# Expert tiles of 128 gathered rows in place of 256, in a routed feed-forward layer

## The chip, the cores and the metric

The kernel runs on 1 core of one Trainium2 chip. The metric is the device time of one execution in microseconds. Before the change the median of 3 runs is 1785.74 us (1784.13 to 1794.47).

## The reference

One block over x of shape (4, 1024, 128), 4096 tokens of width 128, in float32: attention, a feed-forward layer with experts, a state-space scan, and the same feed-forward layer with the same weights again, each on a layer norm of its input and added to it. The change touches the feed-forward layer:

```python
def _L0_ffn_ref(x, sw1, sw2, sw3, ew1, ew2, ew3, rw, rb):
    shared = silu(x @ sw1) * (x @ sw2) @ sw3
    probs = softmax(x @ rw + rb)                  # 8 experts
    w, idx = top_k(probs, 2); w = w / sum(w)
    h = silu(x @ ew1[e]) * (x @ ew2[e])           # 128 -> 256 per expert
    routed = sum over the two chosen e of w * (h @ ew3[e])
    return shared + routed
```

(The matrix products are written as `@` here; the reference computes all experts for all tokens and multiplies by gates that are zero for those not chosen.)

## The kernel before, in words

`build` writes out the stages one behind the other: projection, attention, a second attention branch (`memory`), the first feed-forward layer (`ffn`, stage "ffn1"), the scan ("ssm"), and the second feed-forward layer ("ffn2") with a final `join`. Within a stage each engine has its own program; engines wait for each other by semaphores, and a stage's end waits for all of them.

A feed-forward layer has two parts. `route` (L1576) goes over 8 units of 512 tokens: it normalises them, computes the shared part, picks two experts per token, counts for each pick its place in the expert's region, and POOL scatters the normalised rows with an indirect DMA (`scatter`, L1539; 64 DMAs of 128 rows) into `ex`, a buffer in DRAM with a region for each expert. Each row carries its token number and its gate in two more columns. Zero rows are stored behind each region's end. DVE then writes two small tables (`name_experts`, L1825, and `name_rows`, L1848): for each tile of the next part the expert whose weights it uses and the first row that it reads.

`run_experts` (L1861) goes over `TILES_EX` = 40 tiles of `ROWS` = 256 rows (`SUB` = 2 pieces of 128). That number is fixed: 8192 picked rows make 32 full tiles, and each of the 8 experts may need one more for its remainder. Every tile is computed, those that no expert needs too. The work on a tile:

```python
if on[2]:
    e = pe.value_load(at_expert[0:1, number_of(ti, tq)])
    pe.wait_ge(hid_ready, now(s - 2))
    ...
if on[1]:
    pe.wait_ge(xT_ready, now(s + 0))
    pe.wait_ge(w12_ready, now(s + 0))
    ...
if on[0]:
    pe.wait_ge(loaded[q], now(i * 16 + 16))
```

`pipeline` (L1893) writes the first `AHEAD` steps out, puts the rest into a loop whose turn is `AHEAD` steps, and writes out the last three. In the loop the counts that a step waits for are held in registers (`Turns`, L82; `now`, L131), which L111 and L1953 work out.

Of the kernel before, what the change touches and what calls it, by code (L numbers as in the profile page):

```python
# [30 lines left out]
UPT = UNIT // P  # L31
# [1281 lines left out]
EXPERTS, HIDDEN, TOP = 8, 256, 2  # L1313
HC = HIDDEN // P
TILES_IN = N // P
SUB = 2
ROWS = SUB * P

TILES_EX = TOP * N // ROWS + EXPERTS
# [6 lines left out]
XROW = D + 2  # L1326
TOKEN, GATE = D, D + 1
PADROW = TOP * N
AHEAD = 8
OUTS = 8  # L1330
UNITS_IN = N // UNIT
DEEP = 8
GROUP_ENDS = [1, 3, 5, UNITS_IN]
AHEAD_UNITS, AHEAD_ENDS = 2, [1, 2, 3, 5, 7, UNITS_IN]
EXPERT_STRIDES = [AHEAD, 16, SUB * 16]

def past(s, n):
# [21 lines left out]
class Router:  # L1360
# [22 lines left out]
    def signals(self):  # L1383

        m = self.m
        self.x_loaded = [m.sem(f"x_ld{k}") for k in range(DEEP)]
        self.r_loaded, self.ready, self.set_up, self.stat, self.mean = (m.sem(n) for n in ("r_ld", "ready", "set_up", "stat", "mean"))
# [25 lines left out]
def mean_dve(nc, r, dve, u):  # L1413
    k = u % DEEP
    dve.wait_ge(r.x_loaded[k], u // DEEP * 16 + 16)
    dve.wait_ge(r.mean, u * UPT)
# [11 lines left out]
def norm_dve(nc, r, dve, u):  # L1428
    k = u % DEEP
    dve.wait_ge(r.rstd_ready, sum(end <= u for end in r.ends) + 1)  # L1430
    if u >= DEEP:
        dve.wait_ge(r.sent[k], u // DEEP * (TOP * UPT * 16))
        dve.wait_ge(r.xT_made, u - DEEP + 1)
# [105 lines left out]
def scatter(nc, r, dram, pool, u, j):  # L1539

    k = u % DEEP
    if j == 0:
        pool.wait_ge(r.xn_ready, u * UPT + UPT)
        pool.wait_ge(r.twin_ready, u + 1)
        pool.wait_ge(r.id_ready, u + 1)
        pool.wait_ge(r.gate_ready, u + 1)
        pool.wait_ge(r.pos_ready, u + 1)
    n, j = j // UPT, j % UPT
    nc.gpsimd.indirect_dma_start(dram["ex"], bass.IndirectOffsetOnAxis(ap=r.pos[k][:, n, j:j + 1], axis=0),
                                 r.xn[k][:, n, j, :], None).then_inc(r.sent[k], 16)  # L1550

def rstd_pool(nc, r, pool, g):
# [22 lines left out]
def route(nc, dram, c, a, stage, src, w, w_loaded, t, r):  # L1576

    with ExitStack() as ctx:
        m = Mem(nc, ctx, stage)
        if r is None:  # L1580
            r = Router(m, dram[stage + "_sent"], GROUP_ENDS)
            r.signals()
        first = len(r.x)
# [5 lines left out]
        base = [m.sb(f"base{k}", [P, UPT, D]) for k in range(2)]  # L1589
        zeros = m.sb("zeros", [P, PADS * SUB, XROW])  # L1590
        counti = m.sb("counti", [1, EXPERTS], I32)
# [44 lines left out]
        def pads(eng, sem, experts):  # L1636
            for e in experts:
                n = eng.value_load(counti[0:1, e:e + 1], min_val=0, max_val=N)
                eng.dma_start(dram["ex"][ds(n + e * REGION, ROWS), :].rearrange("(j p) d -> p j d", p=P),
                              zeros[:, e * SUB:(e + 1) * SUB, :]).then_inc(sem, 16)  # L1640

        with nc.Block(no_gpsimd_drain=True) as block:
            @block.sync
            def _(sp):
# [15 lines left out]
                sp.wait_ge(r.ready, 7)  # L1660
                sp.dma_start(dram["ex"][IDLE:ROWS_EX, :].rearrange("(j p) d -> p j d", p=P), zeros[:, EXPERTS * SUB:, :]).then_inc(pads_stored[0], 16)
                for u in range(UNITS_IN):
# [95 lines left out]
            @block.gpsimd  # L1758
            def _(pool):
                if not first:  # L1760
                    set_up_pool(nc, r)
                pool.wait_ge(r.ready, 5)
                group, held = first, first - 1
                if not first:
                    nc.gpsimd.memset(zeros[:], 0.0).then_inc(r.ready, 1)
                if first:
                    for j in range(0, 3):
                        scatter(nc, r, dram, pool, held, j)
                rstd_pool(nc, r, pool, group)
                nc.gpsimd.iota(t["tile"][:], pattern=[[1, TILES_EX], [0, EXPERTS]], base=0, channel_multiplier=0,  # L1770
                               allow_small_or_imprecise_dtypes=True).then_inc(made, 1)
                nc.gpsimd.iota(t["enum"][:], pattern=[[0, TILES_EX], [1, EXPERTS]], base=0, channel_multiplier=0,
                               allow_small_or_imprecise_dtypes=True).then_inc(made, 1)
                nc.gpsimd.memset(t["onesv"][:], 1.0).then_inc(made, 1)
                nc.gpsimd.iota(t["idle"][:], pattern=[[ROWS, TILES_EX]], base=IDLE - FULL * ROWS, channel_multiplier=0,
                               allow_small_or_imprecise_dtypes=True).then_inc(made, 1)
                if first:
                    for j in range(3, 6):
                        scatter(nc, r, dram, pool, held, j)
                rstd_pool(nc, r, pool, group + 1)  # L1780
                if first:
                    nc.gpsimd.memset(zeros[:], 0.0).then_inc(r.ready, 1)
                pool.wait_ge(r.ready, 6)
                nc.gpsimd.iota(zeros[:, :, TOKEN].bitcast(I32), pattern=[[P, PADS * SUB]], base=PADROW, channel_multiplier=1).then_inc(r.ready, 1)
                if first:
                    for j in range(6, TOP * UPT):
                        scatter(nc, r, dram, pool, held, j)
                for u in range(first, UNITS_IN):
                    for j in range(TOP * UPT):
                        scatter(nc, r, dram, pool, u, j)  # L1790
                    if group + 2 + u - first < len(r.ends):
                        rstd_pool(nc, r, pool, group + 2 + u - first)
                for k in range(DEEP):
                    pool.wait_ge(r.sent[k], UNITS_IN // DEEP * TOP * UPT * 16)
        m.leave()
        if r.m is not m:
            r.m.leave()
# [63 lines left out]
def run_experts(nc, dram, c, stage, w, w_loaded, t, base, base_loaded):  # L1861

    with ExitStack() as ctx:
        m = Mem(nc, ctx, stage)
        at_expert, firsti = t["at_expert"], t["firsti"]
        x = [m.sb(f"x{q}", [P, SUB, XROW]) for q in range(AHEAD)]
        xT = [m.sb(f"xT{q}", [P, ROWS]) for q in range(2)]
        w12 = [m.sb(f"w12{q}", [P, 2 * HIDDEN]) for q in range(2)]
        act1 = [m.sb(f"act{q}", [P, HC, ROWS]) for q in range(2)]  # L1870
        hid = [m.sb(f"hid{q}", [P, HC, ROWS]) for q in range(2)]
        out = [m.sb(f"out{q}", [P, SUB, D]) for q in range(OUTS)]
        ps_x = [m.ps(f"ps_x{q}", [P, UNIT]) for q in range(2)]
        ps_h = [[m.ps(f"ps_h{n}{q}", [P, HC, ROWS]) for q in range(2)] for n in range(2)]
        ps_o = [m.ps(f"ps_o{q}", [P, UPT, D]) for q in range(2)]
        step, passed = m.sem("step"), m.sem("passed")
        loaded = [m.sem(f"loaded{q}") for q in range(AHEAD)]
        sent = dram[stage + "_sent"]
# [5 lines left out]
        def number_of(i, q):  # L1884

            return ds(i * AHEAD + q, 1) if not isinstance(i, int) else slice(i * AHEAD + q, i * AHEAD + q + 1)

        def shifted(i, q, by):

            at = q + by  # L1890
            return i + at // AHEAD, at % AHEAD

        def pipeline(body, turns, eng, lag):  # L1893

            deepest = max(lag)
            for s in range(AHEAD):
                body(0, 0, s, [g <= s for g in lag])
# [7 lines left out]
        with nc.Block(no_gpsimd_drain=True) as block:  # L1906
# [76 lines left out]
            def _(act):  # L1983
                turns = Turns(act, stage + "_act", EXPERT_STRIDES, first=1)

                def body(i, at, q, on):
                    s = i * AHEAD + q
                    if on[2]:
                        z, (ti, tq) = (q - 3) % 2, shifted(i, q, -3)
                        act.wait_ge(o_done, now(s - 2))  # L1990
                        if past(s, 3 + OUTS):
                            ui, uq = shifted(i, q, -3 - OUTS)
                            act.wait_ge(sent[uq], now(ui * (SUB * 16) + SUB * 16))
                        for j in range(SUB):
                            nc.scalar.activation(out[tq % OUTS][:, j, :], ps_o[z][:, j, :], ACT.Copy,  # L1995
                                                 scale=x[tq][:, j, GATE:GATE + 1]).then_inc(out_ready, 1)
# [14 lines left out]
            @block.gpsimd  # L2011
            def _(pool):
                m.wipe(pool)
                turns = Turns(pool, stage + "_pool", sorted(set(EXPERT_STRIDES + [SUB * AHEAD])), first=1)

                def body(i, at, q, on):
                    s = i * AHEAD + q
                    for j in range(SUB):
                        pool.wait_ge(out_ready, now(s * SUB + (j + 1)))
                        pool.sem_inc(passed, 1)  # L2020
                        nc.gpsimd.indirect_dma_start(dram["ey"], bass.IndirectOffsetOnAxis(ap=x[q][:, j, TOKEN:TOKEN + 1].bitcast(I32), axis=0),  # L2021
                                                     out[q % OUTS][:, j, :], None).then_inc(sent[q], 16)

                pipeline(body, turns, pool, [0])
                for q in range(AHEAD):
                    pool.wait_ge(sent[q], TILES_EX // AHEAD * SUB * 16)
# [52 lines left out]
def routing_scratch(nc, m, dram, stages):  # L2079

    for name, shape, dt in (("ex", (ROWS_EX, XROW), F32), ("ey", (PADROW + PADS * ROWS, D), F32), ("base", (N, D), F32)):
        dram[name] = nc.dram_tensor(f"{name}_dram", shape, dt).ap()
    for stage in stages:
        dram[stage + "r_sent"] = [m.sem(f"{stage}_sent{k}") for k in range(DEEP)]
        dram[stage + "e_sent"] = [m.sem(f"{stage}_out{q}") for q in range(AHEAD)]

# [836 lines left out]
```

## Time and profile before

| | us |
|---|---|
| median of 3 runs (lowest, highest) | 1785.74 (1784.13, 1794.47) |
| the profiled execution | 1792.23 |
| its span, first to last instruction | 1790.5 |
| PE busy in the span | 1362.6 (76%) |
| DVE busy | 1266.3 (71%) |
| POOL busy | 880.4 (49%) |
| ACT busy | 855.2 (48%) |
| first expert stage, from the first load (L1916) to the start of the last scatter (L2021) | 841.2 to 964.8 |
| second expert stage, from the first xT copy (L2007) to the start of the last scatter | 1643.9 to 1764.1 |

The times of the trace are in microseconds from the span's start. A row for a group of instructions gives the line, the engine, the operation, the tile written and the tiles read, and how many there are.
### The profile page before, as it was taken

How to read it: one execution, taken by the hardware profiler on the slowest of the kernel's cores; microseconds unless marked ns; L12 is line 12 of the kernel's file. 1: busy time of each engine (PE TensorE's matmuls, PEld its weight loads, DVE VectorE, ACT ScalarE, POOL GpSimd, SP SyncE). 2: the span in 40 equal slices, each digit the busy share in tenths (PEclk: the TensorE clock that was granted, in tenths of full speed). 3: DMA queues.
4: the chain of work that ended last, by engine and by line, in shares of the span. 5: the costliest groups of instructions: out<-in, count | busy, mean ns of one | idle time of the engine just before them, and what ended most of it. 6: DMA issues, size and time to landing. Idle time of an engine off the chain costs nothing. (4 is left out here: it accounts for less than half of the span.)

```text
span 1790.5 us, 27815 instructions
## 1 busy us (share of the span) xinstructions
PE 1362.6 (76%) x8207; PEld 677.6 (38%) x8208; DVE 1266.3 (71%) x2981; ACT 855.2 (48%) x1215; POOL 880.4 (49%) x775
## 2 busy tenths in 40 slices
PE   3448999999999898785995777586676544584993
PEld 1213333333333265553994232131221200353992
DVE  3666899999989267674333279998998999573343
ACT  3403666666666734221553668467476332121551
POOL 3400212121211454675665248869869666475662
PEclk9655999999999999997997888698788656797996
DMA  4821111111112232254333395976957863624336
GB/s 121 265 73 48 53 49 55 47 58 44 61 47 65 54 84 84 86 159 108 85 93 111 98 226 154 249 182 162 245 131 199 198 163 94 174 87 124 111 93 166
DMA packets 218312, 210.68 MB, mean 118 GB/s; under 512 B 49247, under 2 KB 188482, under 8 KB 215874
## 3 DMA queue, kind: packets, MB, share of 16 engines
q1 hardware_dynamic: 196174, 180.70, 37.7%
q0 software_dynamic: 9216, 19.02, 3.3%
q10 hardware_dynamic: 12800, 9.46, 1.8%
q8 instruction: 60, 0.98, 0.2%
q14 instruction: 62, 0.51, 0.1%
HBM read 145.27 MB, written 63.37 MB: 117 GB/s over the span
## 5 line engine op out<-in xcount | busy, mean ns | idle before, releaser
L804 ACT ACTIVATE attn_prob<-attn_ps_cols 128x1024 f32<-128x1024 f32 (+1 forms) x320 | 292.0, 940 | 219.7 <-PE attn_ps_cols L680 218.7
L2546 POOL TENSOR_TENSOR ssm_hc<-ssm_h,ssm_cb 128x1024 f32<-128x1024 f32 x128 | 300.5, 2355 | 136.1 <-DVE ssm_h L2529 112.3
L2529 DVE TENSOR_TENSOR_SCAN ssm_h<-ssm_decay,ssm_ps_u 128x1024 f32<-128x1024 f32 x128 | 292.7, 2287 | 29.9 <-ACT ssm_decay L2517 12.6
L830 POOL TENSOR_SCALAR_AFFINE_SELECT attn_prob<-attn_prob 128x512 f32<-128x512 f32 x128 | 81.2, 635 | 415.7 <-ACT attn_prob L804 415.7
L712 DVE CUSTOM_DVE_ANT_0 attn_ps_rows<-attn_ps_rows,const_mask_rows 128x384 f32<-128x384 f32 (+3 forms) x512 | 236.1, 522 | 39.5 <-PE attn_ps_rows L647 37.3
L647 PE MATMUL attn_ps_rows<-attn_ks,attn_qs 72*128 72x512 bf16 (+3 forms) x768 | 228.8, 351 | 44.3 <-DMA attn_qs<-parts_dram 31.0
L2517 ACT ACTIVATE ssm_decay<-ssm_wide,ssm_aneg 128x1024 f32<-128x1024 f32 x128 | 146.1, 1146 | 173.5 <-DVE ssm_h L2529 97.1
L2480 PE MATMUL ssm_ps_u<-ssm_stack,ssm_spread 96*128 96x512 bf16 x256 | 99.1, 479 | 154.0 <-DVE ssm_h L2529 147.4
L680 PE MATMUL attn_ps_cols<-attn_qs,attn_ks 75*128 75x512 bf16 (+3 forms) x768 | 194.3, 333 | 4.6 <-DMA attn_qs<-attn_nrows 3.9
L699 PE MATMUL attn_ps_o<-attn_prob,attn_vw 128*32 128x512 f32 (+3 forms) x1536 | 166.6, 506 | 0.3 <-POOL attn_prob L830 0.3
L717 DVE TENSOR_REDUCE attn_nm<-attn_ps_rows 128x1 f32<-128x512 f32 x256 | 157.8, 682 | 7.8 <-PE attn_ps_rows L647 7.7
L2524 DVE TENSOR_TENSOR ssm_ps_u<-ssm_ps_u,ssm_bb 128x1024 f32<-128x1024 f32 x128 | 154.8, 1209 | 8.7 <-PE ssm_ps_u L2480 8.7
L647 PEld LDWEIGHTS attn_ps_rows<-attn_ks,attn_qs 72*128 72x128 bf16 x768 | 71.4, 100 | 180.4 <-DVE attn_nm L712 65.0
L2480 PEld LDWEIGHTS ssm_ps_u<-ssm_stack,ssm_spread 96*128 96x128 bf16 x256 | 17.3, 103 | 252.9 <-DVE ssm_h L2529 202.7
L680 PEld LDWEIGHTS attn_ps_cols<-attn_qs,attn_ks 75*128 75x128 bf16 x768 | 69.9, 100 | 87.8 <-ACT attn_prob L804 35.5
L2021 POOL DMA_INDIRECT ey_dram<-ffn1e_out,ffn1e_x x80 | 76.6, 957 | 50.9 <-ACT ffn1e_out L1995 38.3
L2021 POOL DMA_INDIRECT ey_dram<-ffn2e_out,ffn2e_x x80 | 76.6, 957 | 50.1 <-ACT ffn2e_out L1995 37.5
L2496 PE MATMUL ssm_ps_y<-ssm_hc,ssm_gather 128*32 128x512 f32 x512 | 83.4, 782 | 7.6 <-POOL ssm_hc L2546 7.6
L1970 PE MATMUL ffn1e_ps_h<-ffn1e_xT,ffn1e_w 128*128 128x256 f32 x320 | 77.6, 386 | 0.9 <-ACT ffn1e_xT L2007 0.9
L1970 PE MATMUL ffn2e_ps_h<-ffn2e_xT,ffn2e_w 128*128 128x256 f32 x320 | 77.1, 384 | 0.9 <-ACT ffn2e_xT L2007 0.9
L1096 DVE TENSOR_TENSOR mem_am<-mem_ps_a,const_strict 128x512 f32<-128x512 f32 x96 | 60.3, 684 | 20.6 <-PE mem_ps_a L1014 20.5
L1940 DVE TENSOR_TENSOR ffn1e_hid<-ffn1e_act,ffn1e_ps_h 128x512 f32<-128x512 f32 x40 | 27.5, 688 | 66.0 <-PE ffn1e_ps_h L1970 66.0
(361 smaller groups left out, 2438.6 us busy)
## 6 DMA issues: line engine op xcount, KB each, us to landing
ssm_wide<-delta_dram SPq DMA_DIRECT2D x128, 512.0 KB, 6.4
attn_ks<-parts_dram SPq DMA_DIRECT2D x48, 192.0 KB
attn_qs<-parts_dram SPq DMA_DIRECT2D x48, 192.0 KB
parts_dram<-proj_parts SPq DMA_DIRECT2D x8, 768.0 KB, 3.8
ffn1e_x<-ex_dram SPq DMA_DIRECT2D x40, 130.0 KB, 2.3
ffn2e_x<-ex_dram SPq DMA_DIRECT2D x40, 130.0 KB, 2.3
split_dram<-ssm_parts SPq DMA_DIRECT2D x6, 768.0 KB, 4.3
ssm_stack<-split_dram SPq DMA_DIRECT2D x18, 256.0 KB, 4.5
```

What stands on the lines that cost most here:

```text
L647: done = nc.tensor.matmul(out[:, x * w:(x + 1) * w], qs[k][0:KROWS, h, blk * P:(blk + 1) * P], ks[k][0:KROWS, h, half * QW:half * QW + w], ...
L680: done = nc.tensor.matmul(out[:, x, 0:w], ks[k][:, h, j * P:(j + 1) * P], qs[k][:, h, at:at + w], start=True, stop=True, skip_group_check= ...
L699: done = nc.tensor.matmul(ps_o[32 * h:32 * h + 32, at - ch * QW:at - ch * QW + w], vw[k % 2][:, j, h, :], prob[u % RING][:, h, 0:w], start ...
L712: done = nc.vector.tensor_tensor_reduce(scores, scores, c["mask_rows"][:, QW - w:], -1.0, -MINUS, ALU.add, ALU.min, into[:, h, at:at + 1])
L717: nc.vector.tensor_reduce(to, ps_rows[bank][:, 0:len(heads) * w].rearrange("p (h w) -> p h w", w=w), AX.X, ALU.max, negate=True).then_inc( ...
L804: nc.scalar.activation(prob[u % RING][:, heads[0]:heads[-1] + 1, 0:w], ps_cols[s % 2][:].rearrange("p b (x q) -> p (b x) q", x=len(heads) ...
L1970: done = nc.tensor.matmul(ps_h[n][z][:, h, :], w12[z][:, n * HIDDEN + h * P:n * HIDDEN + (h + 1) * P], xT[z][:], start=True, stop=True)
L2021: nc.gpsimd.indirect_dma_start(dram["ey"], bass.IndirectOffsetOnAxis(ap=x[q][:, j, TOKEN:TOKEN + 1].bitcast(I32), axis=0), out[q % OUTS][: ...
L2517: nc.scalar.activation(decay[t % DECAY_RING][:], wide[t % WIDE_RING][:], ACT.Exp, scale=aneg[:, at:at + 1]).then_inc(decay_ready, 1)
L2524: nc.vector.tensor_tensor(ps_u[t % 2][:], ps_u[t % 2][:], bb[b % 2][:], ALU.mult).then_inc(dbx_done, 1)
L2529: nc.vector.tensor_tensor_scan(h[t % H_RING][:], decay[t % DECAY_RING][:], ps_u[t % 2][:], 0.0, ALU.mult, ALU.add).then_inc(scan_done, 1)
L2546: nc.gpsimd.tensor_tensor(hc[:, t % HC_RING, :], h[t % H_RING][:], cb[b % 2][:], ALU.mult).then_inc(hc_done, 1)
```

## The change

The tiles of the expert stage have 128 rows in place of 256, so there are 64 + 8 = 72 of them. There are 12 row buffers where there were 8, and 6 result buffers where there were 8 of double size. The loop's turn, which is `AHEAD` steps, becomes 12 steps. The scatters of `route` count on 4 semaphores instead of 8. The zero rows behind each region, the spare rows and the spare places shrink with `ROWS`.

```diff
-SUB = 2
+SUB = 1
 ROWS = SUB * P
 
 TILES_EX = TOP * N // ROWS + EXPERTS
...
-AHEAD = 8
-OUTS = 8
+AHEAD = 12
+OUTS = 6
 UNITS_IN = N // UNIT
 DEEP = 8
+SENT = 4
...
-EXPERT_STRIDES = [AHEAD, 16, SUB * 16]
+EXPERT_STRIDES = [AHEAD, 16]
...
-                                 r.xn[k][:, n, j, :], None).then_inc(r.sent[k], 16)
+                                 r.xn[k][:, n, j, :], None).then_inc(r.sent[u % SENT], 16)
...
-                for k in range(DEEP):
-                    pool.wait_ge(r.sent[k], UNITS_IN // DEEP * TOP * UPT * 16)
+                for k in range(SENT):
+                    pool.wait_ge(r.sent[k], UNITS_IN // SENT * TOP * UPT * 16)
...
-                turns = Turns(pool, stage + "_pool", sorted(set(EXPERT_STRIDES + [SUB * AHEAD])), first=1)
+                turns = Turns(pool, stage + "_pool", EXPERT_STRIDES, first=1)
...
-        dram[stage + "r_sent"] = [m.sem(f"{stage}_sent{k}") for k in range(DEEP)]
+        dram[stage + "r_sent"] = [m.sem(f"{stage}_sent{k}") for k in range(SENT)]
```

Lines behind the new `SENT` are one further down in the changed kernel: L1970 becomes L1971, L1977 becomes L1978, and so on.

On PE, one step of the first expert stage ahead of the loop (the fifth) stood so before. ISA is register work on an address, `ffn_w` is the weight tile of all experts, `ffn1e_w` the copy of one expert's weights, `ffn1e_ps_h` the hidden rows in PSUM; waits aren't shown:

```order
L1953 TENSOR_LOAD ffn_at_expert
L1959 ISA x3
L1959 MATMUL ffn1e_ps_o<-ffn_w,ffn1e_hid 128x128
L1959 ISA x3
L1959 MATMUL ffn1e_ps_o<-ffn_w,ffn1e_hid 128x128
L1959 ISA
L1959 MATMUL ffn1e_ps_o<-ffn_w,ffn1e_hid 128x128
L1959 ISA
L1959 MATMUL ffn1e_ps_o<-ffn_w,ffn1e_hid 128x128
L1970 MATMUL ffn1e_ps_h<-ffn1e_xT,ffn1e_w 128x256 x4
L1977 MATMUL ffn1e_ps_x<-const_ident,ffn1e_x 128x128 x2
```

On PE the same step now:

```order
L1954 TENSOR_LOAD ffn_at_expert
L1960 ISA x3
L1960 MATMUL ffn1e_ps_o<-ffn_w,ffn1e_hid 128x128
L1960 ISA x3
L1960 MATMUL ffn1e_ps_o<-ffn_w,ffn1e_hid 128x128
L1971 MATMUL ffn1e_ps_h<-ffn1e_xT,ffn1e_w 128x128 x4
L1978 MATMUL ffn1e_ps_x<-const_ident,ffn1e_x 128x128
```

Of a step's matmuls two of L1959 go, those of L1970 are half as wide, and one of the two transposes goes; of its register work two single ISA instructions go, and the table read and the two groups of three stay.

On DVE, one step in the loop of the first expert stage stood so before:

```order
L1930 ISA
L1930 TENSOR_LOAD ffn_at_expert
L1933 ISA x3
L1933 COPY ffn1e_w<-ffn_w 128x512
L111 REGISTER_ALU
L1940 TENSOR_TENSOR ffn1e_hid<-ffn1e_act,ffn1e_ps_h 128x512
```

On DVE the same step now:

```order
L1931 ISA
L1931 TENSOR_LOAD ffn_at_expert
L1934 ISA x3
L1934 COPY ffn1e_w<-ffn_w 128x512
L111 REGISTER_ALU
L1941 TENSOR_TENSOR ffn1e_hid<-ffn1e_act,ffn1e_ps_h 128x256
```

The multiplication is half as wide; the table read, the register work and the copy of the weights are as they were, for half the rows.

## Rows read from the trace of the kernel before

**Rows 1.** Stretches of the first expert stage; columns as in the first line.

```profile
core 0: us, PE busy (x) PEld busy (x) DVE busy (x) ACT busy (x) POOL busy (x), PEclk, DMA share, GB/s
840.00:850.00 10.00, 5.60 (x17) 4.07 (x18) 1.97 (x4) 1.36 (x3) 0.00 (x0) 0.59 0.38 94
850.00:860.00 10.00, 10.00 (x65) 9.08 (x64) 3.79 (x7) 5.63 (x14) 4.79 (x5) 1.00 0.21 55
...
900.00:910.00 10.00, 10.00 (x64) 9.11 (x63) 3.79 (x8) 5.61 (x15) 6.70 (x7) 1.00 0.31 86
```

**Rows 2.** Groups of instructions by line and shape, 839 to 975 us.

```profile
L2021 POOL DMA_INDIRECT ey_dram<-ffn1e_out,ffn1e_x x80 | 76.6, 957 | 50.9 <-ACT ffn1e_out L1995 38.3 <-issue 12.3 <-DMA ey_dram<-ffn1e_out,ffn1e_x 0.3
...
L1940 DVE TENSOR_TENSOR ffn1e_hid<-ffn1e_act,ffn1e_ps_h 128x512 f32<-128x512 f32 x40 | 27.5, 688 | 66.0 <-PE ffn1e_ps_h L1970 66.0
L1995 ACT ACTIVATE ffn1e_out<-ffn1e_ps_o,ffn1e_x 128x128 f32<-128x128 f32 x80 | 25.0, 363 | 21.7 <-PE ffn1e_ps_o L1959 21.7
L2002 ACT ACTIVATE ffn1e_act<-ffn1e_ps_h 128x512 f32<-128x512 f32 x40 | 23.9, 597 | 12.2 <-PE ffn1e_ps_h L1970 12.2
L1933 DVE COPY ffn1e_w<-ffn_w 128x512 f32 x40 | 17.1, 429 | 21.1 <-issue 19.0
...
L2007 ACT ACTIVATE ffn1e_xT<-ffn1e_ps_x 128x256 f32<-128x256 f32 x40 | 15.3, 383 | 42.7 <-PE ffn1e_ps_x L1977 42.7
```

**Rows 3.** Timeline, 895 to 903 us, PE: start, length, instructions merged.

```profile
897.40 1.89 PE L1970 MATMUL ffn1e_ps_h<-ffn1e_xT,ffn1e_w 128*128 128x256 f32 x8
...
899.13 0.38 PE L1977 MATMUL ffn1e_ps_x<-const_ident,ffn1e_x 128*128 128x128 f32 x2
...
899.35 1.06 PE L1959 MATMUL ffn1e_ps_o<-ffn_w,ffn1e_hid 128*128 x8
...
900.24 1.89 PE L1970 MATMUL ffn1e_ps_h<-ffn1e_xT,ffn1e_w 128*128 128x256 f32 x8
```

**Rows 4.** One step of PE's sequencer (duration ns, first and last start); ACT's copy before.

```profile
L1975 PEldq EVENT_SEMAPHORE  x1: 51/51/51, 914.3 to 914.3; - x1
L1953 PEldq FUSED_REGOPS  x1: 51/51/51, 914.4 to 914.4; - x1
L1953 PEldq TENSOR_LOAD <-ffn_at_expert x1: 305/305/305, 914.5 to 914.5; - x1
L111 PEldq ALU_OP  x2: 32/32/32, 914.9 to 916.0; - x2
...
L1959 PEldq FUSED_REGOPS  x4: 37/105/173, 915.0 to 915.7; - x4
L1959 PEldq SEQ_ASSERT  x4: 18/18/18, 915.2 to 915.9; - x4
...
L1967 PEldq EVENT_SEMAPHORE  x1: 51/51/51, 916.1 to 916.1; - x1
...
913.83 0.39 ACT L2007 ACTIVATE ffn1e_xT<-ffn1e_ps_x 128x256 f32<-128x256 f32 x1 [0.56 <-PE ffn1e_ps_x L1977]
```

**Rows 5.** The same two waits in a step with the loop's turn.

```profile
L1975 PEldq EVENT_SEMAPHORE  x1: 51/51/51, 885.8 to 885.8; - x1
...
L1967 PEldq EVENT_SEMAPHORE  x1: 51/51/51, 888.2 to 888.2; - x1
```

**Rows 6.** First and last start of xT copies and scatters, first stage.

```profile
L2007 ACT ACTIVATE ffn1e_xT<-ffn1e_ps_x x40: 383/383/388, 844.2 to 956.4; 128x256 f32<-128x256 f32 x40
...
L2021 POOL DMA_INDIRECT ey_dram<-ffn1e_out,ffn1e_x x80: 954/957/964, 853.3 to 964.8; - x80
```

**Rows 7.** L1970 in the first tile, 843.4 to 848.5 us.

```profile
L1970 PE MATMUL ffn1e_ps_h<-ffn1e_xT,ffn1e_w x8: 551/634/793, 844.6 to 847.8; 128*128 128x256 f32 x8
```

**Rows 8.** SP's first eight loads, 840 to 850.2 us.

```profile
L1916 SPq DMA_DIRECT2D ffn1e_x<-ex_dram x8: 378/378/416, 841.2 to 849.2; - x8
...
DMA to landing us min/median/max: 2.0/2.1/2.2
```

**Rows 9.** Scatters, the last table's cast, and POOL's waits, 756 to 776 us.

```profile
L1549 POOL DMA_INDIRECT ex_dram<-ffn1r_xn,ffn1r_pos x48: 954/958/1113, 774.9 to 837.4; - x48
...
L1858 DVE CAST ffn_firsti<-ffn_first x2: 172/252/333, 825.6 to 1621.6; 1x40 int32<-1x40 f32 x2
...
POOL ex_dram L1549 <- DVE ffn1r_xn L1436: 3.6, 1, 3.6
```

**Rows 10.** A stretch of the second routing; columns as in rows 1.

```profile
1610.00:1620.00 10.00, 7.46 (x34) 4.08 (x33) 8.45 (x31) 2.41 (x5) 7.56 (x9) 1.00 0.42 123
```

## The prediction

> **What bounds the kernel now.** I read the expert stage first in stretches of 10 us, then by groups of instructions, then one tile in order of time, and last the register work of TensorE's own sequencer. The reader is to see in [rows 1] that from 850 us on PE is busy in every microsecond at the full granted clock, so the stage is PE's. [rows 2] show the other engines far below it: per tile of 256 rows ACT has 0.38 + 0.60 + 2 x 0.36 = 1.71 us, DVE 0.43 + 0.69 = 1.12 us, POOL two scatters of 0.96 us with 0.3 us of issue each (12.3 us over 40 tiles), 2.5 us. [rows 3] give the beat: L1970 starts at 897.40 and again at 900.24, so 2.84 us per tile, in the order L1970, L1977, L1959. The passes inside are evenly spaced: with 256 columns (1.89 - 0.38) / 7 = 0.216 us apart, with 128 columns (1.06 - 0.275) / 7 = 0.112 us.
>
> What a busy PE hides is in [rows 4]: the sequencer of TensorE (PEldq) waits at L1975, reads the expert number (305 ns), does register work for the two weight addresses at L1959, and reaches the wait of L1967 at 916.1, 1.8 us later, 1.9 us to that wait's end. Nothing in it waits: the durations are 51 + 51 + 305 + 2 x 32 + 4 x 105 + 4 x 18 + 51 = 1.01 us, and the rest over 14 instructions is 0.06 us between one and the next. [rows 5] show the same stretch where the loop turns, 885.8 to 888.2: 0.5 us more. Against a beat of 2.84 us this work costs nothing now; it has 0.9 us to spare. In every tile it starts anew just behind xT: the copy of [rows 4] ends at 913.83 + 0.39 = 914.22, L1975 runs at 914.3.
>
> **The change, term by term.** PE's streaming falls. A tile of 128 rows has 8 passes of L1970, now of 128 columns, 4 passes of L1959 and one of L1977, at 0.112 us: 1.45 us, and 72 of them are 104 us where 40 x 2.84 is 114 us. That would be 9 us gained per stage, if streaming still set the beat.
>
> It does not, by [rows 4]. The order of instructions shows that a tile still reads the expert number and still does the three-step register work for both address halves; only the two single checks of the second half tile go (SEQ_ASSERT, 18 ns each, with 0.08 us of gaps and the issue of one matmul each). That is 0.2 us of 1.9, so 1.7 us are left per tile. Behind them come the issue of L1971's passes and the return to the wait before L1978. That stretch is always cut short by a wait in the trace, so I bound it: not below 0, and not above 0.25 us, four times the usual gap. The nearest row is the step from L1975 to L1953 in [rows 4], 0.1 us with two matmuls in it; I take 0.1. With 0.5 us per loop turn, now one in 12 tiles, 0.04 us, the beat is 1.84 us in the loop. The first 12 tiles are written out, without the L111 and L1953 register steps (0.3 us); their table reads run while loads are landing, so I take 1.7 us. Thus 9 x 1.7 + 60 x 1.84 = 125.7 us for the last 69 beats, 1.82 us each.
>
> The ends of the stage gain. [rows 6]: ACT's first xT starts at 844.2 and the last at 956.4, and POOL's last scatter starts 8.4 us after that, at 964.8. At the start the clock is low [rows 1], and the 8 passes of the first tile run from 844.6 to 847.8, 0.43 us each [rows 7]. With half the columns they take half: 1.7 us, with transpose and copy 2.5 us for each of the first two beats. A half tile is also turned 0.2 us sooner. So the last xT starts at about 844.0 + 2 x 2.5 + 125.7 = 974.7. The tail is one tile of half the rows and one scatter in place of two queued ones: copy 0.3, L1971 1.2, the multiplication 0.4, L1960 with its register work 1.3, ACT 0.4, issue 0.2, 3.8 us. The last scatter starts at 978.5 where it was 964.8: 13.7 us later. The second stage has the same 40 tiles, and its output goes on to the join just as the first's goes on to the scan, both behind the last scatter; I count it as equal. **Sum: +27 us.** The profiled execution took 1792.2 us (span 1790.5, 1.7 around it), so 1819 for that one; it stood 6.5 us above the median of the runs, 1785.7, so I predict 1813 us.
>
> Edits that I put at nothing, with what covers them. Row buffers, 8 x 256 to 12 x 128: SP issued its eight loads without a wait 1.14 us apart [rows 8], so even with a wait for the scatter added (one more register step, 0.1 to 0.2 us) it keeps below 1.82 and stays several tiles ahead. Without that lead PE would wait for a landing, 2.1 us [rows 8]. Six result buffers: POOL needs 0.96 + 0.3 = 1.26 us per scatter, below the beat. DVE copies an expert's weights 72 times where it was 40 (0.43 us each, [rows 2]); with the half multiplication that is under 0.9 us per tile, and with its own table reads (about 0.8 us, DVE does the same reads as PE) still below 1.3. If one of these exceeded 1.82 us it would set the beat. ACT per tile, from 0.60 for 512 and 0.38 for 256 columns: 0.28 + 0.38 + 0.36 = 1.02 us. The larger tables of expert numbers (72 entries for 40) are written by DVE at 825.6 while POOL scatters until 837.4 [rows 9]. The smaller zero block and larger iotas fall on POOL before a wait of 3.6 us for DVE [rows 9]: no gain, no loss. Four scatter semaphores for eight: the same waits at the end.
>
> **Rivals.** *The round trip decides.* Per tile PE streams L1971, transposes the next tile, ACT copies xT, and only then may L1971 go on: 8 x 0.112 + 0.11 + 0.30 (last transpose to copy) + 0.28 + 0.06 = 1.64 us. It lies beside the register work, so it decides if that takes under 1.64 us. Then 69 x 1.64 = 113.2 us replaces 125.7: +1.2 us per stage, +2 in all, 1788 us. For it speaks that these rows are exact; against it, that [rows 4] leave 1.7 us at the least.
>
> *The other side: streaming decides.* If the register work ran ahead under queued passes, and the transposes of a later tile too, the beat would be PE's 1.45 us: 844.0 + 5.0 + 69 x 1.45 + 3.8 = 952.9, 12 us earlier per stage, 24 in all: 1762 us. It takes over as soon as both chains above fall under 1.45 us. For it: busy 10.00 of 10 in [rows 1]. Against it: the order puts L1978 behind L1971, and the sequencer's place just behind the copy in [rows 4]. The Trainium skill (Advanced Engine Details and Errata, Sequencer Loop) speaks for this rival: it lets other engine instructions be read and queued while control work executes. By that rule the register work would vanish and the time would be this rival's; the trace agrees only in part, since work runs ahead as far as the next waiting matmul (L1975 at 914.3, behind the copy's end at 914.22).
>
> *The clock falls.* PE would idle 0.4 us in each 1.82. At the low clock 13 passes take 0.213 us (half of [rows 7]), 2.8 us per tile, 69 x 1.0 us more than with register work deciding, 81 us per stage: about 1950 us. Against it: from 1610 to 1620 PE was busy 7.46 of 10 us at the full clock [rows 10]. The Trainium skill (TensorE: Matmul & The Clock Gate, Part 1: The HAM clock gate) says that the clock is halved after idling and so speaks against short work with gaps; the trace agrees on the low clock after idling (0.59 in the first stretch of [rows 1]), and that row shows gaps that did not lower it.
>
> **How the numbers follow.** A measurement of this kernel tells about 1% (18 us) from no change. Register work decides 0.72, round trip 0.14, streaming 0.10, low clock 0.04. Within the first, the beat may lie between 1.70 flat (+5.3 us per stage, 1796 us) and 1.95 (+22.6, 1831 us); below a beat of 1.75 the loss is under 18 us, which I give 0.12. So slower 0.60 + 0.04 = 0.64, within 1% 0.12 + 0.14 = 0.26, faster 0.10. The range runs from the round trip's 1788 to the upper end, 1787 to 1832.
>
> **What would show it.** Right: in the loop xT copies start 1.8 us apart, PE idles 0.3 to 0.4 us per tile with "issue" or nothing named, the sequencer's stretch from L1976 to L1968 takes 1.7 us and starts with no wait, POOL waits for ACT in each tile, and the last scatter of the first stage starts near 978 us. If copies come 1.64 us apart and L1976 again runs just behind them, it was the round trip; at 1.45 us with PE busy throughout, streaming; SP or DVE at work without idle time would mean that I mispriced one of them. The prediction is wrong altogether if the two expert stages together change by less than 18 us.

## The result, and the profile after

The changed kernel takes 1823.11 us in the median of 4 runs (1816.70 to 1831.99), the kernel before 1785.45 us beside it: a ratio of 1.0183, 95% interval 1.0154 to 1.0212. It is slower by 1.8%, on the side that was forecast and within the range given. The profiled execution took 1826.53 us, its span 1824.8; that is 34.3 us longer than the span before, where the sum had put 27.

The expert stage in two stretches (columns as in [rows 1], which these answer):

```profile
850.00:860.00 10.00, 9.95 (x80) 9.25 (x79) 5.99 (x12) 5.97 (x18) 5.27 (x6) 1.00 0.37 91
900.00:910.00 10.00, 9.65 (x69) 8.19 (x69) 5.12 (x11) 5.16 (x16) 5.64 (x6) 1.00 0.28 73
```

The clock is still granted in full. PE's busy share hardly fell, from 10.00 to 9.65, and by it alone the stage would still look bound by streaming. The timeline shows where the column misleads (start, length, as in [rows 3]):

```profile
899.60 0.91 PE L1960 MATMUL ffn1e_ps_o<-ffn_w,ffn1e_hid 128*128 x4
899.74 0.28 ACT L2008 ACTIVATE ffn1e_xT<-ffn1e_ps_x 128x128 f32<-128x128 f32 x1 [0.17 <-PE ffn1e_ps_x L1978]
...
900.34 1.06 PE L1971 MATMUL ffn1e_ps_h<-ffn1e_xT,ffn1e_w 128*128 128x128 f32 x8
...
901.23 0.27 PE L1978 MATMUL ffn1e_ps_x<-const_ident,ffn1e_x 128*128 128x128 f32 x1
901.39 0.91 PE L1960 MATMUL ffn1e_ps_o<-ffn_w,ffn1e_hid 128*128 x4
...
901.54 0.28 ACT L2008 ACTIVATE ffn1e_xT<-ffn1e_ps_x 128x128 f32<-128x128 f32 x1 [0.17 <-PE ffn1e_ps_x L1978]
901.70 0.96 POOL L2022 DMA_INDIRECT ey_dram<-ffn1e_out,ffn1e_x  x1 [0.84 <-ACT ffn1e_out L1996]
902.14 1.06 PE L1971 MATMUL ffn1e_ps_h<-ffn1e_xT,ffn1e_w 128*128 128x128 f32 x8
```

L1971 starts at 900.34 and 902.14: 1.80 us per tile. The four passes of L1960 take 0.91 us; at 0.112 us apart they would take 3 x 0.112 + 0.275 = 0.61. The 0.3 us between them is time in which PE has no work, but the records cover it with longer matmuls (up to 372 ns, where all took 275 before). The xT copy is done at 901.54 + 0.28 = 901.82, and L1971, which waits for it, starts 0.32 us later. Where the copy does release it, it follows at 0.05 us (experiment 1), so something else does so here. (The Trainium skill says, in Perfetto Trace Analysis, Identifying the Most-Contended Engine, that the matmul busy share is no good measure of how near TensorE is to its limit; here it stood at 9.65 while another chain set the beat.)

That chain is PE's sequencer, by lines, from 899 to 903 us for the first two rows and from 900.25 to 902.0 for the others (they answer to [rows 4]):

```profile
L1976 PEldq EVENT_SEMAPHORE  x2: 51/51/51, 900.3 to 902.1; - x2
L1968 PEldq EVENT_SEMAPHORE  x2: 51/51/51, 900.1 to 901.9; - x2
...
L1954 PEldq FUSED_REGOPS  x1: 51/51/51, 900.4 to 900.4; - x1
L1954 PEldq TENSOR_LOAD <-ffn_at_expert x1: 306/306/306, 900.5 to 900.5; - x1
...
L1957 PEldq EVENT_SEMAPHORE  x1: 51/51/51, 900.9 to 900.9; - x1
...
L1960 PEldq FUSED_REGOPS  x4: 37/105/173, 901.0 to 901.7; - x4
L1960 PEldq SEQ_ASSERT  x2: 18/18/18, 901.2 to 901.6; - x2
```

From L1976 at 900.3 to L1968's end at just under 902.0 it works without a wait, and L1976 of the next tile runs at 902.1. It no longer stands just behind the copy, as it did before; it runs back to back. As L1968 still comes 0.1 us behind the copy's end, these rows by themselves leave the round trip in play; experiments 1 and 2 settle it.

The ends of the two stages (by line: shortest, median and longest in ns, first and last start; they answer to [rows 6]):

```profile
L2008 ACT ACTIVATE ffn1e_xT<-ffn1e_ps_x x72: 277/277/278, 844.5 to 975.4; 128x128 f32<-128x128 f32 x72
L2008 ACT ACTIVATE ffn2e_xT<-ffn2e_ps_x x72: 277/277/278, 1661.2 to 1793.2; 128x128 f32<-128x128 f32 x72
...
L2022 POOL DMA_INDIRECT ey_dram<-ffn1e_out,ffn1e_x x72: 952/957/1111, 851.0 to 980.3; - x72
L2022 POOL DMA_INDIRECT ey_dram<-ffn2e_out,ffn2e_x x72: 952/957/966, 1668.6 to 1798.1; - x72
```

The last scatter of the first stage starts at 980.3 where it was 964.8, 15.5 us later. From first copy to last scatter the stages take 135.8 and 136.9 us where they took 120.6 and 120.2.

### The profile page after: what moved, and what is told of

It is laid out like the page before. It is cut to its first block and busy times, and to the rows that moved or that the text cites. A ratio compares the mean times of both kernels' runs of the same rounds, so it can differ in the third digit from the quotient of the medians.

```text
span 1824.8 us, 30671 instructions
## 1 busy us (share of the span) xinstructions
PE 1399.0 (77%) x8639; PEld 697.8 (38%) x8640; DVE 1319.2 (72%) x3109; ACT 874.7 (48%) x1327; POOL 866.2 (47%) x759
## 5 line engine op out<-in xcount | busy, mean ns | idle before, releaser
L2547 POOL TENSOR_TENSOR ssm_hc<-ssm_h,ssm_cb 128x1024 f32<-128x1024 f32 x128 | 300.8, 2357 | 136.3 <-DVE ssm_h L2530 112.2
L2481 PE MATMUL ssm_ps_u<-ssm_stack,ssm_spread 96*128 96x512 bf16 x256 | 95.4, 463 | 149.4 <-DVE ssm_h L2530 143.6
L2022 POOL DMA_INDIRECT ey_dram<-ffn2e_out,ffn2e_x x72 | 69.0, 958 | 73.8 <-ACT ffn2e_out L1996 70.4
L2022 POOL DMA_INDIRECT ey_dram<-ffn1e_out,ffn1e_x x72 | 69.1, 960 | 72.6 <-ACT ffn1e_out L1996 66.2
L1971 PE MATMUL ffn2e_ps_h<-ffn2e_xT,ffn2e_w 128*128 128x128 f32 x576 | 78.7, 281 | 0.7 <-ACT ffn2e_xT L2008 0.7
L1971 PE MATMUL ffn1e_ps_h<-ffn1e_xT,ffn1e_w 128*128 128x128 f32 x576 | 78.0, 279 | 0.7 <-ACT ffn1e_xT L2008 0.7
L1934 DVE COPY ffn2e_w<-ffn_w 128x512 f32 x72 | 38.7, 538 | 49.6 <-issue 32.8
```

Of the source, the lines that this page charges most:

```text
L1971: done = nc.tensor.matmul(ps_h[n][z][:, h, :], w12[z][:, n * HIDDEN + h * P:n * HIDDEN + (h + 1) * P], xT[z][:], start=True, stop=True)
L2547: nc.gpsimd.tensor_tensor(hc[:, t % HC_RING, :], h[t % H_RING][:], cb[b % 2][:], ALU.mult).then_inc(hc_done, 1)
```

## The experiments

All ratios are to the kernel before, on the same chip (medians of 1791.9 to 1792.2 us there). The changed kernel was timed where the kernel before took 1785.45 us, so a difference between its 1823.11 us and the time of an experiment is uncertain by 6 to 7 us; the beats in the traces do not have this uncertainty.

**1. The range checks gone.** The address of a weight slice costs three register steps in front of its matmul: a first of 173 ns, a range check of 18 ns (SEQ_ASSERT) and a last of 37 ns. With the number's range given (expert numbers are 0 to 7) and its check left out, one step is left.

```diff
-e = pe.value_load(at_expert[0:1, number_of(ti, tq)])
+e = nc.values_load(at_expert[0:1, number_of(ti, tq)], engines=[mybir.EngineType.PE],
+                   min_val=0, max_val=(EXPERTS - 1) * EW, skip_runtime_bounds_check_because=...)
```

> The changed kernel with the range checks of PE's two weight addresses gone: of the three register steps ahead of each address one is left, so about 2 x 0.3 us of register work go per tile; the result is the same. Register work decides (my theory): in the loop xT copies come 1.80 us apart now; they fall to the round trip's 1.64 and no further, and the loop's turns (2.38 now) fall by about 0.5, 12 us less per stage, about 1799 us in all. Round trip decides already: no change, 1823. Another engine decides (POOL, SP or DVE, none of which is touched): no change, 1823. Streaming decides: no change.

Measured: 1798.02 us, ratio 1.0032 (1.0016 to 1.0047). PE's sequencer, by line, from 900.3 to 902 us:

```profile
L1961 PEldq FUSED_REGOPS  x2: 46/46/46, 900.9 to 901.1; - x2
```

ACT's copies and PE in the timeline:

```profile
901.22 0.61 PE L1961 MATMUL ffn1e_ps_o<-ffn_w,ffn1e_hid 128*128 x4
901.42 0.28 ACT L2009 ACTIVATE ffn1e_xT<-ffn1e_ps_x 128x128 f32<-128x128 f32 x1 [0.17 <-PE ffn1e_ps_x L1979]
901.75 1.16 PE L1972 MATMUL ffn1e_ps_h<-ffn1e_xT,ffn1e_w 128*128 128x128 f32 x8
...
903.06 0.28 ACT L2009 ACTIVATE ffn1e_xT<-ffn1e_ps_x 128x128 f32<-128x128 f32 x1 [0.17 <-PE ffn1e_ps_x L1979]
```

Two steps of 46 ns are left of six. L1961 is back at 0.61 us, and L1972 starts at 901.75, 0.05 us behind the copy's end at 901.70. Copies come 1.64 us apart: the round trip decides now, at the length worked out for it. By line the copies of both stages:

```profile
L2009 ACT ACTIVATE ffn1e_xT<-ffn1e_ps_x x72: 277/278/278, 844.0 to 962.4; 128x128 f32<-128x128 f32 x72
L2009 ACT ACTIVATE ffn2e_xT<-ffn2e_ps_x x72: 277/278/278, 1647.4 to 1767.3; 128x128 f32<-128x128 f32 x72
```

From first to last copy they take 118.4 and 119.9 us where the changed kernel takes 130.9 and 132.0. Some 25 us went with steps that never touch data; the kernel is still not faster than the one before.

**2. The transposes early.** PE's block for L1978 moves ahead of the block for L1971, so that ACT copies xT(s) while PE streams the products of tile s-1.

```diff
 (L1960, tile s-3)
+if on[0]: ... transpose of tile s
 if on[1]: ... L1971, tile s-1
-if on[0]: ... transpose of tile s
```

> The changed kernel with PE's transposes of tile s issued ahead of the products with the first two weights of tile s-1 instead of behind them: the round trip through ACT's copy is then covered by 0.9 us of streaming; PE's register work stays. Register work decides: beats in the loop stay at 1.80 us (within 0.03), only the ten or so written out ahead of the loop, now 1.64, may fall to 1.5; 1819 to 1823 us. Round trip decides: beats fall to streaming's 1.45, 24 us less per stage, about 1775 us. Another engine decides: no change.

Measured: 1822.02 us, ratio 1.0159 (1.0140 to 1.0177). The timeline of ACT:

```profile
906.09 0.27 ACT L2008 ACTIVATE ffn1e_xT<-ffn1e_ps_x 128x128 f32<-128x128 f32 x1
907.89 0.27 ACT L2008 ACTIVATE ffn1e_xT<-ffn1e_ps_x 128x128 f32<-128x128 f32 x1
```

The beat stays at 1.80 us with the round trip out of the way. So it does not decide in the changed kernel, and register work does.

**3. Both edits.**

> The two edits together (no range checks on PE's addresses, transposes early). Register work decides: both chains behind PE are now below its streaming, so beats fall to 1.45 to 1.50 us (the upper end where DVE, whose register work of 0.85 us and copy of 0.57 us follow one another, is next), 21 to 25 us less per stage than 1823: 1773 to 1781 us, faster than the kernel before. Another engine decides (POOL's scatter with its issue, SP, DVE): beats stay at 1.8, 1823. If the low clock follows from the gaps instead, the granted clock in the stage would be below 1.00 in one of the runs.

Measured: 1775.79 us, ratio 0.9906 (0.9885 to 0.9926): faster than both kernels. By line the copies of the first stage:

```profile
L2009 ACT ACTIVATE ffn1e_xT<-ffn1e_ps_x x72: 271/272/277, 842.2 to 947.5; 128x128 f32<-128x128 f32 x72
```

The timeline of PE:

```profile
901.18 1.06 PE L1979 MATMUL ffn1e_ps_h<-ffn1e_xT,ffn1e_w 128*128 128x128 f32 x8
902.07 0.61 PE L1961 MATMUL ffn1e_ps_o<-ffn_w,ffn1e_hid 128*128 x4
...
902.52 0.27 PE L1969 MATMUL ffn1e_ps_x<-const_ident,ffn1e_x 128*128 128x128 f32 x1
902.63 1.06 PE L1979 MATMUL ffn1e_ps_h<-ffn1e_xT,ffn1e_w 128*128 128x128 f32 x8
```

The stretch that answers to 900 to 910 us of the changed kernel:

```profile
900.00:910.00 10.00, 10.00 (x93) 10.00 (x92) 5.94 (x14) 6.29 (x22) 6.48 (x8) 1.00 0.30 86
```

1.45 us per tile, 13 x 0.112: streaming decides in the loop, and the gain that smaller tiles offer is there. POOL, SP, DVE and the buffers were not touched, so in the first stage none of them has a floor above 1.45 us; in its loop only the beats at the turn (1.62 to 1.68) and right behind it (up to 1.50) are longer. In the second stage one beat takes 4.30 us: PE waits for the load of the thirteenth tile, the first that SP issues behind the 2 MB that it loads for the join. The clock stays in full behind it (a row of the timeline, and a stretch with columns as in [rows 1]):

```profile
1653.52 0.33 PE L1969 MATMUL ffn2e_ps_x<-const_ident,ffn2e_x 128*128 128x128 f32 x1 [2.56 <-DMA ffn2e_x<-ex_dram]
1654.00:1656.00 2.00, 2.00 (x21) 2.00 (x20) 0.59 (x2) 1.07 (x4) 0.00 (x0) 1.00 0.24 59
```

Twelve buffers, with which the changed kernel never waits for this load, no longer hide it here. PEld is the column that tells this kernel from the changed one, 10.00 against 8.19. The Trainium skill's rule (Advanced Engine Details and Errata, Sequencer Loop) that engine instructions are queued while control work runs is borne out here: the register work runs under queued passes at no cost. Experiment 2 shows the other half: the control work is one chain, and where it is longer than the streaming it sets the beat.

**4. The number read twice.** The opposite dose: one more table read per tile in PE's register work.

```diff
-e = pe.value_load(at_expert[0:1, number_of(ti, tq)])
+e = [pe.value_load(at_expert[0:1, number_of(ti, tq)]) for _ in range(HC)]
...
-flat[:, ds(e + (2 * HIDDEN + h * D), D)]
+flat[:, ds(e[h] + (2 * HIDDEN + h * D), D)]
```

> The changed kernel with PE reading the expert's number twice per tile, once for each address: one more table read (0.31 us and a gap of 0.06) in its register work, nothing else. Register work decides: every beat in the loop grows by 0.37, to 2.17, and the written-out ones to 1.9 or less, 24 us more per stage, about 1871 us. Round trip decides, with the register work just below it (1.64): some 0.2 us per beat, 1850. Another engine decides, with PE's register work beside it: no change up to its slack.

Measured: 1882.45 us, ratio 1.0504 (1.0477 to 1.0531). The copies by line:

```profile
L2008 ACT ACTIVATE ffn1e_xT<-ffn1e_ps_x x72: 277/277/278, 848.1 to 1005.8; 128x128 f32<-128x128 f32 x72
```

The same stretch:

```profile
900.00:910.00 10.00, 8.61 (x58) 7.05 (x59) 4.52 (x10) 4.41 (x14) 4.79 (x5) 1.00 0.19 53
```

The mean beat is (1005.8 - 848.1) / 71 = 2.22 us where it was (975.4 - 844.5) / 71 = 1.84: 0.38 more, which is what a read and its gap take. From first to last copy the stages take 26.8 and 25.6 us more than in the changed kernel, where 24 had been put; the time is 11 us above the 1871 that were expected, of which some 4 us are in these beats. The clock stayed at 1.00 with PE at 8.61.

**5. The same read in the kernel before.**

> The kernel before (256 rows) with the edit of the run that read the expert's number twice: one more table read per tile in PE's register work, which cost the changed kernel 0.4 us per tile. Register work hidden below the streaming in the kernel before (my theory, 0.9 us to spare): no change, xT copies stay 2.84 us apart, within 3 us of the kernel before. If register work costs its time wherever it stands: 0.4 us x 40 tiles x 2 stages, 32 us slower.

Measured: 1794.76 us, ratio 1.0011 (0.9986 to 1.0036). By line:

```profile
L2007 ACT ACTIVATE ffn1e_xT<-ffn1e_ps_x x40: 384/384/387, 848.0 to 960.5; 128x256 f32<-128x256 f32 x40
```

112.5 us from the first copy to the last where it was 112.2 [rows 6]. The step that costs 52 us in the beats of the small tiles costs nothing that can be measured in the time with large ones. In the trace it shows only where the loop turns: copies start at 891.74 and 894.87 there, 3.13 us apart, where the kernel before has 2.92. The chain of 1.9 us, with 0.5 for the turn and 0.4 for the read, comes near the beat of 2.84 there, and some 0.2 us come through.

**6. Both edits in the kernel before.**

> The kernel before (256 rows) with the two edits that took the changed kernel below it: no range checks on PE's addresses, transposes early. If the kernel before is bound by streaming, as I read it, they bring nothing there: beats stay at 2.84 us, within 4 us of the kernel before (the first beats may gain 1 us). If the two edits are a gain of their own, apart from the smaller tiles, they bring up to the 10 to 16 us by which the kernel with both stood below the one before.

Measured: 1790.57 us, ratio 0.9982 (0.9963 to 1.0001). By line:

```profile
L2008 ACT ACTIVATE ffn1e_xT<-ffn1e_ps_x x40: 377/378/384, 843.5 to 954.3; 128x256 f32<-128x256 f32 x40
```

110.8 us for 39 beats, 2.84 each; the 1.4 us went from the first two beats. The gain of experiment 3 thus needs the smaller tiles: they bring it, once their own register work is out of the way.

**7. Eight buffers.** The smaller tiles with the buffer counts of before (`SENT` stays at 4).

```diff
-AHEAD = 12
-OUTS = 6
+AHEAD = 8
+OUTS = 8
```

> The changed kernel with 8 row buffers and 8 result buffers, so with the smaller tiles alone; the loop's turn is again 8 steps. If the buffers were put at nothing rightly: 8 turns per stage where there are 5, at 0.55 to 0.65 us each, and 4 tiles more in the loop at 0.17 us more each, 2.5 us per stage, 5 us in all: about 1827 us, with SP's loads still ahead of PE. If twelve row buffers are needed to cover the loads (2.2 us from a scatter's issue to its landing, 1.8 for a load): PE waits for landings in the loop, and beats are above 1.80.

Measured: 1832.50 us, ratio 1.0232 (1.0180 to 1.0283); the profiled one took 1828.0. Its interval overlaps that of the changed kernel (1.0154 to 1.0212), so the times do not tell the two apart; the traces do. PE waits for a landing in the second stage and not in the first. The copies by line:

```profile
L2008 ACT ACTIVATE ffn1e_xT<-ffn1e_ps_x x72: 277/278/278, 843.3 to 975.3; 128x128 f32<-128x128 f32 x72
L2008 ACT ACTIVATE ffn2e_xT<-ffn2e_ps_x x72: 277/278/278, 1657.0 to 1793.5; 128x128 f32<-128x128 f32 x72
```

PE in the timeline of the second stage:

```profile
1674.50 0.33 PE L1978 MATMUL ffn2e_ps_x<-const_ident,ffn2e_x 128*128 128x128 f32 x1 [1.74 <-DMA ffn2e_x<-ex_dram]
```

Two stretches there:

```profile
1674.00:1678.00 4.00, 2.80 (x16) 2.49 (x17) 0.54 (x2) 1.04 (x4) 0.46 (x2) 0.84 0.26 67
1678.00:1682.00 4.00, 4.00 (x26) 3.80 (x26) 1.47 (x4) 2.03 (x6) 1.54 (x2) 0.73 0.30 81
```

In the first stage the 71 beats take 132.0 us where they took 130.9, 1.1 us for three more turns where 2.5 had been put, and PE waits for no load. In the second they take 136.5 where they took 132.0: PE waits 1.74 us for the load of the ninth tile. SP, from 1660 to 1676 us, had waited before that load for the scatter that last used the buffer to land:

```profile
SPq L1915 <- DMA ey_dram<-ffn2e_out,ffn2e_x: 8.0, 1, 8.0
```

The scatters issued in these microseconds land after 5.2 us in the median, where it was 2.2 in the first stage (848 to 862 us). The join's 2 MB, issued right ahead at 1662.55, are on their way for 11.0 us; that they delay the scatter is likely, but was not tried by itself. That in experiment 3, with twelve buffers, it is the thirteenth tile that waits, again the first behind these 2 MB, speaks for it. Behind PE's wait the granted clock falls; in stretches of 2 us from 1674 on it is 1.00, 0.69, 0.50, 0.96.

**8. DVE's range checks gone too**, on top of experiment 3, by the same edit at L1931.

> The kernel with both edits (1775.8 us) with the range check gone from DVE's weight copies too. If PE's streaming sets the 1.45 us beat there: no change in the loop, within 3 us of 1776. If DVE's chain (register work and copy one after the other, about 1.42 us) still decides in some beats, those at the loop's turn (1.65) above all: 0.1 to 0.2 us per turn, 1 to 3 us in all.

Measured: 1775.19 us, ratio 0.9907 (0.9873 to 0.9942), the same as without it. DVE does not decide at 1.45 us, and not at the loop's turn, where the beats stay at 1.62 to 1.65.

## Why the prediction was right

*Register work decides.* The likeliest case came about. Experiments 1, 2 and 4 show it from three sides: less of it is faster, taking the round trip off the path is not, more of it is slower one for one. 5 and 6 show that it was hidden in the kernel before.

*The terms.* By the starts of copies number 1, 3, 12 and 72 in the first stage, which the next rows complete, the last scatter comes about as follows:

```profile
849.35 0.28 ACT L2008 ACTIVATE ffn1e_xT<-ffn1e_ps_x 128x128 f32<-128x128 f32 x1 [0.20 <-PE ffn1e_ps_x L1978]
...
864.35 0.28 ACT L2008 ACTIVATE ffn1e_xT<-ffn1e_ps_x 128x128 f32<-128x128 f32 x1 [0.17 <-PE ffn1e_ps_x L1978]
...
975.42 0.28 ACT L2008 ACTIVATE ffn1e_xT<-ffn1e_ps_x 128x128 f32<-128x128 f32 x1 [0.17 <-PE ffn1e_ps_x L1978]
...
976.15 1.06 PE L1971 MATMUL ffn1e_ps_h<-ffn1e_xT,ffn1e_w 128*128 128x128 f32 x8
...
979.12 0.37 ACT L1996 ACTIVATE ffn1e_out<-ffn1e_ps_o,ffn1e_x 128x128 f32<-128x128 f32 x1 [0.94 <-PE ffn1e_ps_o L1960]
...
980.27 0.96 POOL L2022 DMA_INDIRECT ey_dram<-ffn1e_out,ffn1e_x  x1 [0.35 <-issue]
```

| term, us | predicted | measured |
|---|---|---|
| first copy starts | 844.0 | 844.5 |
| first two beats | 5.0 | 4.8 |
| nine beats ahead of the loop | 15.3 | 15.0 |
| sixty beats in the loop | 110.4 | 111.1 |
| last copy to last scatter | 3.8 | 4.9 |
| last scatter starts | 978.5 | 980.3 |

The loop's beat is 111.1 / 60 = 1.85 where 1.84 was put. That the first two beats fit is in part luck: each was put at 2.5 us, and they take 2.65 and 2.17. Ahead of the loop the mean is 1.67: it was right by the size and not quite by the cause, since the shortest of these beats are 1.63 us, the round trip's length, which there is as long as the register work.

*Mis-sized: the tail.* It took 1.1 us more. Most of that is the term "issue 0.2": POOL starts its scatter 980.27 - 979.49 = 0.78 us behind the end of ACT's multiplication. The price came from the 0.3 us of issue in [rows 2], which is what is left where one scatter stands queued behind another. Another 0.3 us lie ahead of the last L1971, which starts 0.45 us behind the copy's end at 975.70; the sum let it follow at once.

*Counted as equal: the second stage.* It grew by 136.9 - 120.2 = 16.7 us, 1.5 more than the first. Its 71 beats take 132.0 us, 1.1 more, nearly all of it in the second and third: 2.65 and 2.17 us where the first stage has 2.17 and 1.64, with the clock still at 0.50 from 1664 to 1666 us. The two stages together grew by 31.9 us where 27.4 was worked out. Of the 34.3 us, 1.8 are in the stretch from the first stage's last scatter to the second's first copy, 680.9 us where it was 679.1. In the eight other kernels, which have the same work there, it took 675.7 to 681.8: no effect of the change can be read from it. The forecast of 1813 us lies 10 us under the measured median: 7 of them are this sum, 34.3 for 27, and 3 the step from the profiled execution to the median, where 6.5 us were taken off and the changed kernel's differ by 3.4.

*Put at nothing.* POOL, DVE, SP and ACT were rightly left out: in the first stage of experiment 3 all four keep up with 1.45 us. The first copy starts at 844.5 for 844.2; as it starts at 839.1 to 848.1 in the eight other kernels, an effect of the larger tables below some us can't be read. The row buffers were rightly put at nothing for twelve of them at 1.80 us; with eight, or with twelve at 1.45 us, PE waits for a load in the second stage.

*The rivals.* The round trip lay 0.16 us below the register work, and streaming 0.19 us below that; experiments 1 and 3 come down to them one after the other. The clock did not fall from gaps of 0.3 us in 1.80, as the argument from [rows 10] had it; it did fall in experiment 7, behind stops of PE of 1.74 and 0.70 us, and stayed at 1.00 in experiment 3 behind one of 2.56 us. What makes the difference is open.

*What would show it.* One sign failed: idle time of 0.3 to 0.4 us per tile does not stand in PE's rows, as the records of L1960 take it in. The beat of the copies and the sequencer's rows did show it.

## What to carry to other kernels

Work per tile that does not shrink with the tile (a table read, register steps for a dynamic address, a loop's turn) has to be listed by engine and summed as one chain before tiles are made smaller; that it is hidden now says only that the tile is large enough. Where such a chain decides, take steps out of it before anything else: here range checks, for a number whose range is known, were 25 us, and only together with the earlier transposes did the smaller tiles pay. Judge a chain by the beat of what it releases, not by the busy share of the engine.

## What was not expected

- An address with its check costs 173 + 18 + 37 ns in steps and some 0.2 us in gaps; without it one step of 46 ns is left.
- DVE's copy of an expert's weights, the same instruction on the same 128x512, takes 568 ns in the median of the changed kernel's first stage, where it took 427 before, and takes 427 again in experiment 1, whose tiles are as small and whose beat is shorter. It cost nothing, as DVE does not decide. The traces show a pattern: in the changed kernel's loop the copy takes 0.65 to 0.67 us when it starts 0.5 us behind the start of a scatter on POOL, 0.55 to 0.58 at 0.6, 0.46 or 0.47 at 0.7, and 0.43 from 0.8 on. In experiment 1 most copies start 0.8 us behind or later, in the kernel before most start at 0.2 or earlier, and take 0.43. That the scatter holds the copy up is likely; it was not tried.

A copy and the scatter ahead of it in the changed kernel's timeline:

```profile
899.90 0.96 POOL L2022 DMA_INDIRECT ey_dram<-ffn1e_out,ffn1e_x  x1 [0.84 <-ACT ffn1e_out L1996]
...
900.51 0.57 DVE L1934 COPY ffn1e_w<-ffn_w 128x512 f32 x1 [0.43 <-issue]
```

By line, in the changed kernel and then in experiment 1:

```profile
L1934 DVE COPY ffn1e_w<-ffn_w x72: 426/568/671, 842.4 to 974.3; 128x512 f32 x72
```

```profile
L1934 DVE COPY ffn1e_w<-ffn_w x72: 426/427/673, 841.8 to 961.6; 128x512 f32 x72
```
